# Causal attention on one core: statistics of later batches in pairs of tiles, a new order of the units, and the expert stage's loads issued from the attention stage

## The reference

```python
x = L0_attn_x
x = x + _L0_attn_ref(_layernorm(x, axis=-1), L0_attn_Wq, L0_attn_Wk, L0_attn_Wv)
x = x + _L0_ffn_ref(_layernorm(x, axis=-1), L0_ffn_Wg, ..., L0_ffn_down_embed, L0_ffn_up_embed)
...
# _L0_attn_ref
q = jnp.einsum('bte,hed->bhtd', x, Wq)
...
scores = jnp.where(causal, jnp.einsum('bhtd,bhsd->bhts', q, k), -jnp.inf) / jnp.sqrt(E)
out = jnp.einsum('bhts,bhsd->bhtd', softmax(scores), v)
```

## Time and profile before

| | us |
|---|---|
| median of three runs | 4173.62 |
| lowest and highest | 4170.66, 4175.27 |
| the profiled execution | 4178.98 |
| its span | 4177.1 |
| attention stage, to the last output's statistics | about 1166 |

### The profile page before, as it was taken

The page is one execution under the profiler, slowest core; times in us unless marked ns, Lnnn a source line. Parts: engine busy times, 40 slices in busy tenths (PEclk is TensorE's granted clock), DMA queues, the critical chain, the costliest instruction groups (busy, mean ns, idle before and its releaser), DMA issues. The chain is left out here.

```text
span 4177.1 us, 65914 instructions
## 1 busy us (share of the span) xinstructions
PE 3942.8 (94%) x23476; PEld 2362.2 (57%) x23476; DVE 2784.8 (67%) x5635; ACT 2640.7 (63%) x3262; POOL 1554.6 (37%) x1303
## 2 busy tenths in 40 slices
PE   7999999999968999999999989997999999999999
PEld 4455445554447788787887855554444444444444
DVE  7888778887668878878788545445545555554553
ACT  2566666666765545545455334444888888888888
POOL 3222222222334534435344211111555455455545
PEclk7999999999989999999999999999999999999999
DMA  7553444344142232332323210004666766667674
GB/s 180 129 113 75 103 99 104 91 112 111 29 121 76 61 106 77 80 103 61 109 74 84 84 35 1 1 1 106 154 154 154 163 146 154 154 148 159 148 160 99
DMA packets 205761, 429.98 MB, mean 103 GB/s; under 512 B 47584, under 2 KB 72560, under 8 KB 189056
## 3 DMA queue, kind: packets, MB, share of 16 engines
q1 hardware_dynamic: 193360, 411.56, 41.1%
q0 software_dynamic: 4160, 6.35, 0.6%
q10 hardware_dynamic: 7920, 7.87, 0.6%
HBM read 338.59 MB, written 87.03 MB: 102 GB/s over the span
## 5 line engine op out<-in xcount | busy, mean ns | idle before, releaser
L2202 ACT ACTIVATE gelu_out<-hidden,b_col 128x1024 f32<-128x1024 f32 x1024 | 1054.4, 1117 | 181.7 <-PE hidden L2125 176.0
L2185 POOL TENSOR_TENSOR combined<-combined,gated 128x512 f32<-128x512 f32 x480 | 621.5, 1295 | 647.4 <-DVE gated L2302 471.2
L663 DVE TENSOR_REDUCE maxima<-front_and_scoresT 128x1 f32<-128x512 f32 (+3 forms) x1280 | 725.6, 628 | 97.2 <-PE front_and_scoresT L471 61.7
L563 ACT ACTIVATE probsT<-front_and_scoresT 128x1024 f32<-128x1024 f32 (+3 forms) x768 | 599.4, 812 | 236.0 <-PE front_and_scoresT L498 229.8
L1127 POOL TENSOR_TENSOR pair_sums<-sims 128x1024 f32<-128x1024 f32 x256 | 482.9, 1902 | 668.3 <-DVEq L1259 412.5
L2302 DVE SCALAR_TENSOR_TENSOR gated<-out_bank,b_col,gates_spread 128x512 f32<-128x512 f32 x480 | 360.1, 750 | 511.5 <-PE out_bank L2133 482.6
L2125 PE MATMUL hidden<-slice_stack,w_stack 128*128 128x512 f32 x2048 | 622.9, 428 | 37.2 <-ACT gelu_out L2202 36.9
L1055 PE MATMUL dense<-xnT,dense_weights 128*128 128x512 f32 x2304 | 537.3, 395 | 12.7 <-ACT silu_down L1161 8.6
L2125 PEld LDWEIGHTS hidden<-slice_stack,w_stack 128*128 128x128 f32 x2048 | 354.5, 190 | 326.9 <-ACT gelu_out L2202 250.6
L2133 PE MATMUL out_bank<-gelu_out,w_sb 128*32 128x512 f32 x4096 | 517.5, 608 | 2.4 <-DVE combined L2302 2.2
L1055 PEld LDWEIGHTS dense<-xnT,dense_weights 128*128 128x128 f32 x2304 | 435.2, 190 | 112.8 <-ACT silu_down L1161 9.0
(11 more groups left out here) (205 smaller groups left out, 5063.3 us busy)
## 6 DMA issues: line engine op xcount, KB each, us to landing
gates_spread<-gate_scratch SPq DMA_DIRECT2D x512, 256.0 KB, 5.5
dense_weights<-dense_scratch SPq DMA_DIRECT2D x384, 256.0 KB, 2.8
stack_scratch<-split_parts SPq DMA_DIRECT2D x192, 256.0 KB, 3.2
slice_stack<-slice_scratch SPq DMA_DIRECT2D x128, 256.0 KB, 8.2
q_stack<-stack_scratch SPq DMA_DIRECT2D x64, 384.0 KB, 6.3
k_stack<-stack_scratch SPq DMA_DIRECT2D x64, 384.0 KB, 9.2
slice_scratch<-slice_parts SPq DMA_DIRECT2D x32, 512.0 KB, 5.9
out_x<-x_tiles ACTq DMA_DIRECT2D x15, 512.0 KB, 2.9
```

The costliest lines, as they stand in the source:

```text
L563: nc.scalar.activation(PT[:, i % NPT, 2 * pr:2 * pr + 2, at:BANK], R[:, low:high + 1:high - low, at:BANK], ACT.Exp, scale=SCALE).then_inc( ...
L663: nc.vector.tensor_reduce(dst, bank(k)[:, 0:parts * w].rearrange("p (a k) -> p a k", a=parts), AX.X, ALU.max)\
L2185: nc.gpsimd.tensor_tensor(CM[:, par, hc, :], CM[:, par, hc, :], Y[:, u % 2, :], ALU.add)\
L2202: nc.scalar.activation(GH[:, k % GHB, :, :], HP[k % HPB][:, :, :], ACT.Gelu, bias=b1c[:, n % E:n % E + 1])\
```

## The change

- The statistics of batches 5 to 7 are taken two tiles at a time, behind each of the outputs 12 to 23; the scales begin behind output 25 and end behind output 29.
- The strings FIRST, ODD, EVEN, LAST_BUT_ONE and LAST are new. Each step has the same units as before, except that step 0 takes its w letters and m letters in another place.
- A class `EarlyWeights` holds two buffers for both stages, one for the projection weights of the attention and later Wq and the keys, one for the transposed x and later down_embed and up_embed. SP issues the loads of Wq, keys and down_embed at the end of step 14's string, once the last w unit has been read.
- `ln_scales` is split into a first part, a root and a last part, and these stand inside `expert_weights`: on VectorE the first part ahead of the clearing of KB, the last part between the copies and the subtractions. up_embed and bd, which reuse the early buffers, are loaded behind the stores of down_embed's parts.

```diff
@@ strings, STEPS @@
-    EVEN = ("svsmvsmsmmsmvsmsvsmmstwmsswxxmsmvvmmsvsxoxsvssmvxmsxmsmsxoxsmmmpmpmsvvsmsmmspsvtsmsvvsmsvsmssvms"
-            "mpssmvvmosvmsmvmssvmsosmsvsmsvsmsvsm")
+    EVEN = ("smsvmvsmmsmwmsmvsvssmsswxtsmsxvvmsmvmsmvmssvmsmxxsmsosvsssvmssvxoxsmsvvsmsxxmvsmsvsmmmsopsmpsmvv"
+            "mmmpstpsmsvmsmvssmovsmsvmsmvssmvssmm")
...
@@ causal_attention @@
-        STATS_AT = {3: 5, 4: 6, 5: 7}
-        LN_AT = 4 * 6
+        TILES_AT = 2
+        STATS_AT = {12 + k: 5 * KT + TILES_AT * k for k in range((B - 5) * KT // TILES_AT)}
+        LN_AT = 28
...
                 if n + 2 < NS:
                     load_stacks(n + 2, 1)
+                if n + 2 == NS:
+                    sp.wait_ge(freed[True], NFREE[KF["w", NS - 1, 1]])
+                    early.load(sp)
...
-                if unit[0] == "o" and unit[1] % 4 == 0 and unit[1] // 4 in STATS_AT:
-                    stats(STATS_AT[unit[1] // 4])
-                if unit == ("o", LN_AT - 2):
+                if unit[0] == "o" and unit[1] in STATS_AT:
+                    for t in range(STATS_AT[unit[1]], STATS_AT[unit[1]] + TILES_AT):
+                        if t % KT == 0:
+                            dve.wait_ge(later_in[t // KT - 1], 16)
+                        tile_stats(nc, X, STATS, t)
+                if unit == ("o", LN_AT - 3):
                     ln_begin(2)
...
@@ expert_weights @@
             def _(sp):
-                later_loads(sp)
+                small_loads(sp)
                 for b in range(NB):
                     sp.wait_ge(copied_dve, copies(NC + b))
                     sp.dma_start(dense.scratch[b], DP[:, b, :, :, :].bitcast(F32)).then_inc(dense.down_stored, 16)
+                sp.wait_ge(filled, NC + NB)
+                up_load(sp)
...
-                pe.wait_ge(loaded, 16 * (DC + 3))
+                pe.wait_ge(early.prep_in, 16 * (DC + 2))
...
+                pe.wait_ge(early.down_in, 16)
                 for b in range(NB):
...
+                ln_begin(nc, dve, STATS, MEAN, var_ready)
                 nc.vector.memset(KB[:, :, :, :], 0.0).then_inc(zeroed, 1)
...
+                ln_end(nc, dve, STATS, RS, var_ready, sd_ready)
                 for b in range(NB):
                     dve.wait_ge(high, b + 1)
...
             def _(act):
+                ln_root(nc, act, STATS, var_ready, sd_ready)
                 act.wait_ge(zeroed, 1)
...
@@ expert_ffn @@
-        ln_scales(nc, STATS, MEAN, RS, "f0", loads)
-        expert_weights(nc, WQ, KY, DN, prep_in, MT, DP, WQT, KB, ident, later_loads, dense_w)
+        expert_weights(nc, STATS, MEAN, RS, early, MT, DP, WQT, KB, ident, small_loads, up_load, dense_w)
```

More of the change, by code:

```diff
@@ L225, in sem @@
             return ctx.enter_context(nc.semaphore(name))
-        wq = sb("wq_sb", [P, DC, 2, HS, HH])
-        wk = sb("wk_sb", [P, DC, 2, HS, HH])
-        wv = sb("wv_sb", [P, DC, H, HS])
+        wq, wk = (early.small[:, i, :].rearrange("p (c f d h) -> p c f d h", c=DC, f=2, d=HS) for i in range(2))
+        wv = early.small[:, 2, :].rearrange("p (c h d) -> p c h d", c=DC, h=H)
         IH = sb("ident_halves", [P, 2, P], BF16)
         MH = sb("mask_halves", [P, P], BF16)
-        XT = sb("xnT", [P, DC, T])
+        XT = early.rows
         V = sb("values", [P, 2, KT, HH * HV + 32 - HV])
@@ L340, in _ @@
             load_batch(sp, 0, x_in, 2)
-            for w, dst in ((Wq, PT[:, 0, 0, :]), (Wk, PT[:, 0, 1, :]), (Wv, wv[:, :, :, :].rearrange("p c h d -> p (c h d)"))):
+            for w, dst in ((Wq, PT[:, 0, 0, :]), (Wk, PT[:, 0, 1, :]), (Wv, early.small[:, 2, :])):
                 for c in range(DC):
@@ L867, in expert_ffn @@
         DW = sb("dense_weights", [P, dense_w.SLOTS, 2, DC, P], F32R)
-        UP = sb("up_sb", [P, NB, D])
+        UP = early.rows_of
         wd = sb("wd_sb", [P, FB, D])
@@ L878, in expert_ffn @@
         SD = sb("silu_down", [P, NB, TM])
-        GS = sb("silu_gate", [P, 2, TM])
         HT = sb("hiddenT", [P, FB, TM])
-        T8 = sb("top_pairs", [P, TT * H, TOPK])
-        TD = sb("top_less_max", [P, TT * H, TOPK])
+        small = early.small[:, :, :].rearrange("p i n -> p (i n)")
+        GS = small[:, 0:2 * TM].rearrange("p (i t) -> p i t", i=2)
+        T8, TD = (small[:, 2 * TM + i * P:2 * TM + (i + 1) * P].rearrange("p (g k) -> p g k", k=TOPK) for i in range(2))
+        bdr = small[:, 2 * TM + 2 * P:2 * TM + 2 * P + D]
         NMX = sb("neg_max", [P, TT * H])
@@ L2349, in program @@
         dense = DenseParts(nc, ctx, a["L0_ffn_Wg"], a["L0_ffn_Wu"])
-        causal_attention(nc, a["L0_attn_x"], X, STATS, MEAN, RS, B, a["L0_attn_Wq"], a["L0_attn_Wk"],
-                         a["L0_attn_Wv"], ident, dense)
-        expert_ffn(nc, X, STATS, MEAN, RS, B, *(a["L0_ffn_" + n] for n in (
-            "Wg", "bg", "Wu", "bu", "Wd", "bd", "Wq", "keys", "down_embed", "up_embed")), ident, dense)
+        with ExitStack() as shared:
+            early = EarlyWeights(nc, shared, a["L0_ffn_Wq"], a["L0_ffn_keys"], a["L0_ffn_down_embed"])
+            causal_attention(nc, a["L0_attn_x"], X, STATS, MEAN, RS, B, a["L0_attn_Wq"], a["L0_attn_Wk"],
+                             a["L0_attn_Wv"], ident, dense, early)
+            expert_ffn(nc, X, STATS, MEAN, RS, B, *(a["L0_ffn_" + n] for n in (
+                "Wg", "bg", "Wu", "bu", "Wd", "bd", "up_embed")), ident, dense, early)
         later = MixtureWeights(nc, ctx, *(a["L1_ffn_" + n] for n in (
```

139 lines of the change are left out of this document (77 added, 62 removed).

## The result

The changed kernel takes 4205.31 us (median of 6 runs, 4197.08 to 4213.05), the kernel before beside it 4172.14 (6 runs, 4158.43 to 4185.74). The ratio is 1.0080, 95% interval 1.0055 to 1.0104: it is slower by 23 to 43 us. In a later set it was 4205.66 against 4183.96, ratio 1.0054 (1.0035 to 1.0073), which is 15 to 31 us. The forecast was 4197, slower by 24.

The account below looks back on a forecast made before the run. TensorE, busy 94% of the span, was taken as the bound. Terms -5.3 - 9.5 + 23 + 13 + 2.7 = +23.9 us on the median 4173.62 gave 4197.5; range 4153 to 4208.

Parts of the forecast that it names:

- main case: Whole kernel: longer stack-load waits and lower clock outweigh the gains, +23.9 us to 4197.5, own range 4185 to 4210; chance 0.48.
- the rival with the queue that does not bite: SP's queue in even steps: data ready below p3 + 18.5, no step longer; faster, 4159 (4149 to 4165); chance 0.32.
- The stack loads, +23: Six even steps: p3's stores wait behind the row-maxima exchange, each TensorE wait grows 3.84 us; +23 us, bounds 0 and +29.
- The clock, +13: After six stack waits of 4 to 7 us: lower TensorE clock, 2.7 us each, less 2.9 already paid; bounds 0 and +16.
- The first step, +2.7: First step's 4.66 us wait for row maxima behind step 2's stack loads: fewer o, v and s units stand between; +2.7 us.
- The rest of the order, 0: All else in the new order: same units on each engine, taken as 0 us, bounds -8 and +8.
- The statistics, -9.5: VectorE statistics, two tiles behind each of twelve outputs: bursts' TensorE waits and lost clock go; -9.5 us, bounds -12 and -6.
- The expert stage, -5.3: Start of expert stage: early loads bring the first copy 7.2 us sooner, less 1.9 for the scales' second part; -5.3 us.

## Why the prediction was right, point by point

The forecast was 4197, the main case's own range 4185 to 4210, and the time 4205. The mechanism it named is there, and the rival with the queue that does not bite is not. That the total came so near is in part luck: one term was too small and another too large by about as much. By its own steps:

- **The stack loads, +23.** The waits grew by 24.1 us (7.6 to 31.7). The working gave p3's stores a delay of 4.3 us, so loads at p3 + 12.2; they start at p3 + 12.3. It had TensorE at p3 + 18.5; it comes at 18.2. Whether the second half's loads slow the first, which was the upper bound of 29, stays open. Start to ready is 11.3 us on average in this profile with the second half issued 1.9 us behind the first in the step shown, and 11.4 before; but it is 11.5 with the strings alone and 12.0 in the second profile of the changed kernel, where the waits grew by 28.8, against 11.0 to 11.7 in five kernels with the old order. The Trainium skill (DMA: Bandwidth & Descriptors, Queues, rings and completion order) does say that descriptors are consumed in ring order on each DMA engine, but also that a later one may finish its write before an earlier one. So it spoke for +23 less firmly than I took it to, and no run here tests it.
- **The clock, +13: the term that was too small.** The old order with the rest of the change has a clock loss of 11.0 us, the changed kernel 39.6 (43.4 in its second profile), so +28.6; in the kernel before the strings alone took it from 18.4 to 53.1. The price of 2.7 us a wait was read from waits of before, at 166.85 and 992.61, behind which projection products stand. In the new order other units stand behind m0, and the clock stays low for 3.9 to 18.0 us behind the six waits. It was the row's neighbourhood, not its length, that I should have matched. That the products behind the wait matter is a reading of rows in all traces; no run changed them alone, and what makes the clock return early behind two of the six waits is not known.
- **The first step, +2.7.** 5.3. The store stood behind the stack loads for 10.9 us in place of 7.3; I had counted only TensorE's shorter way.
- **The rest of the order, 0: it was a gain of about 20 us**, and this hid the clock's error. From 60 us to the last output the changed kernel has 22.6 us more idle time of TensorE than the old order (30.5 to 53.1) and 16.3 us more busy time (1060.15 to 1076.46), together the 38.9 us by which the last output is later (1150.61 to 1189.55). The waits for the two DMA rows rise by 29.9, so about 7 us of other waits went. The busy time rose by only 16.3 where the clock loss rose by 28.6; with like order the two go together (above), so about 12 us of busy time went with the new order, by a cause that these rows don't show. The order as a whole: 38.7 forecast, 37 measured alone, 38 to 49 on top of the rest.
- **The statistics, -9.5.** Alone 8.2 us between first and last output, 12.5 by the ratio (8 to 17).
- **The expert stage, -5.3.** 5.6. The first twelve similarity products stayed at 5.05 us, as the sum assumed, for a nearer reason than the one given: under the transposes the clock was at 0.50, as by the Trainium skill (TensorE: Matmul & The Clock Gate, Part 4: PE-mode transpose) it should be, and it rose when the matrix products at 1201.72 ran. It was 1.00 from 1204 to 1206. The idle 2.71 us before 1206.93 took it down again.

What would have shown it wrong was named, and didn't come: no step has waits near 1 us with outputs at 133 us; eight outputs take 138 to 147 us between output 8 and output 48, where 138 to 141 was forecast; the clock is what was forecast too small.

## What to carry to other kernels

Where an order is written by hand, list for each transfer what is ahead of it on its queue at the moment its data is ready, and for each engine what it needs first behind it; of three other ways through SP's queue one gave back 10 us and two little or nothing, since they only chose which transfer comes late. Price a wait with the clock that follows it, from a row with the same work behind it. And when a unit moves, keep the buffers' assignment as it was, or check it anew: one letter cost about 26 us through the ring of banks.

## What the runs showed of the hardware

- The store of 32 KB takes from the start of its issue to its landing 1.5 us with nothing ahead of it, 3.75 behind p stores (the step shown above), 7.6 and 11.4 behind the loads of the stacks in the first step (before and after). Its size is the same each time; what was issued before it is not.
- Waits of 4.5 to 6.5 us with small products behind them left the clock at the lower level for 3.9 to 18.0 us of busy work; waits of 7.9 to 9.6 us with projection products behind them gave it back within 6.5 us. So the longer waits cost less beyond themselves.
- 59 waits of half a microsecond did not lower the clock: its loss was 10.8 us with them and 11.0 in the old order without them.
